# Experts of a mixture layer: the shared expert by chunks, the chosen one by gathered tiles

## The reference

```python
# Fourier attention, per head of 16 features
kv = jnp.cumsum(fft(k) * fft(v), axis=1)
vals = ifft(kv * conj(fft(q))).real ; return vals @ w_out
# mixture: swiglu(x, wg, wu, wd) = silu(x @ wg.T) * (x @ wu.T) @ wd.T, 128 -> 256 -> 128
shared_out = swiglu(x, shared_gate, shared_up, shared_down)
logits = x @ gate_w.T                        # 8 experts
top_id = argmax(logits) ; score = sigmoid(max(logits))
routed_out = sum over e of swiglu(where(top_id == e, x * score, 0), r_gate[e], r_up[e], r_down[e])
return shared_out + routed_out
```

## Time and profile before

| | |
|---|---|
| Median of 3 runs | 1799.72 us (1798.75 to 1801.79) |
| The profiled execution | 1799.19 us |
| its span | 1797.3 us |
| PE busy | 1580.2 us (88%) |
| DVE busy | 1324.0 us (74%) |
| ACT busy | 1146.9 us (64%) |
| POOL busy | 713.0 us (40%) |
| Mean granted clock of PE | 0.942 of full |

### The profile page before, as it was taken

One profiled execution on the slowest core, in us unless ns is written; L12 is line 12 of the kernel. 1 busy time (PEld: TensorE's weight loads), 2 busy tenths in 40 slices (PEclk: granted clock), 3 DMA queues, 4 the chain that ended last, 5 costly groups with the idle time before them and its releaser, 6 DMA issues. The chain is left out here.

```text
span 1797.3 us, 35515 instructions
## 1 busy us (share of the span) xinstructions
PE 1580.2 (88%) x8576; PEld 870.8 (48%) x8577; DVE 1324.0 (74%) x3585; ACT 1146.9 (64%) x2294; POOL 713.0 (40%) x1011
## 2 busy tenths in 40 slices
PE   2899999999999999999499999999498973799996
PEld 1333333333333333333277777777345552566664
DVE  2899999999999999998257666666347763466665
ACT  1387888888888888888466666666236553344342
POOL 2223344344443333322413333333135776144444
PEclk8699999999999999999799999999799985899998
DMA  3333332232323233221010000000120112222210
GB/s 110 75 96 100 86 95 79 81 89 77 93 80 87 79 93 95 72 55 31 13 65 1 1 0 0 0 0 1 27 71 16 44 48 97 72 59 59 59 55 17
DMA packets 84446, 102.48 MB, mean 57 GB/s; under 512 B 15995, under 2 KB 49537, under 8 KB 84368
## 3 DMA queue, kind: packets, MB, share of 16 engines
q1 hardware_dynamic: 78992, 88.89, 17.6%
q0 software_dynamic: 5376, 12.66, 2.0%
HBM read 61.44 MB, written 35.33 MB: 54 GB/s over the span
## 5 line engine op out<-in xcount | busy, mean ns | idle before, releaser
L827 DVE TENSOR_REDUCE bmax<-PS 128x8 f32<-128x512 f32 x1024 | 651.3, 683 | 61.4 <-PE PS L568 58.8
L678 ACT ACTIVATE EX<-PS 128x512 f32<-128x512 f32 x1024 | 565.2, 604 | 107.5 <-PE PS L579 97.9
L568 PE MATMUL PS<-KR,QR 33*128 33x512 f32 x1024 | 411.2, 469 | 50.4 <-DVE bmax L827 31.3
L579 PE MATMUL PS<-QR,KR 64*128 64x512 f32 x1024 | 399.1, 460 | 1.6 <-ACT EX L678 1.5
L568 PEld LDWEIGHTS PS<-KR,QR 33*128 33x128 f32 x1024 | 167.0, 188 | 366.6 <-DVE bmax L827 299.3
L589 PE MATMUL PS<-EX,VS 128*9 128x512 f32 x2048 | 268.6, 596 | 1.2 <-ACT EX L678 1.2
L579 PEld LDWEIGHTS PS<-QR,KR 64*128 64x128 f32 x1024 | 162.5, 185 | 11.3 <-ACT EX L678 10.2
L1024 PE MATMUL PS<-pA,wb 128*128 128x512 f32 x640 | 157.0, 401 | 0.0
L763 POOL TENSOR_TENSOR m_diff<-m_prev,m_all 128x16 f32<-128x16 f32 x64 | 14.2, 222 | 328.1 <-DVE m_all L839 328.1
L1853 ACT ACTIVATE g<-PS 128x512 f32<-128x512 f32 x72 | 43.0, 597 | 142.1 <-PE PS L1813 142.1
L1024 PEld LDWEIGHTS PS<-pA,wb 128*128 128x128 f32 x640 | 120.3, 191 | 27.5
(11 more groups left out here) (227 smaller groups left out, 2821.0 us busy)
## 6 DMA issues: line engine op xcount, KB each, us to landing
QR<-q_scr SPq DMA_DIRECT2D x256, 64.0 KB, 2.4
KR<-k_scr SPq DMA_DIRECT2D x256, 64.0 KB, 2.3
k_scr<-partsB SPq DMA_DIRECT2D x42, 256.0 KB, 2.9
rows<-row_scr SPq DMA_DIRECT2D x72, 129.0 KB, 2.1
q_scr<-partsB SPq DMA_DIRECT2D x28, 256.0 KB, 3.0
X<-in_L_attn_x SPq DMA_DIRECT2D x16, 256.0 KB, 3.0
X<-x SPq DMA_DIRECT2D x16, 256.0 KB, 2.4
xB<-in_L_attn_x SPq DMA_DIRECT2D x14, 256.0 KB, 3.3
```

The source lines that it names most:

```text
L568: pe.matmul(PS[:, bank_of(i, n), :], QR[rows, i, h // 2, t * P:(t + 1) * P], KR[rows, i, h // 2, :], start=True, stop=True).then_inc(tile_ ...
L579: pe.matmul(PS[:, RING3 + bank_of(j, n), :], KR[rows, j, h // 2, kt * P:(kt + 1) * P], QR[rows, j, h // 2, :], start=True, stop=True).then ...
L678: act.activation(EX[:, n % (2 * HG), :], PS[:, RING3 + bank_of(j, n), :], ACT.Exp, scale=SCALE).then_inc(ex_set, 1)
L827: dve.tensor_reduce(bmax[:, i % 2, n, :], PS[:, bank_of(i, n), :].rearrange("p (b k) -> p b k", k=BLK), AX_X, ALU.max).then_inc(tile_max, 1)
```

## The change

1. The rows in `row_scr` have 129 floats: the normalised token times its score, and its number. The score goes into a buffer of its own.
2. The chunk stage and the tile stage are one program. The normalised rows are written straight into AO, their transposes into XT (`copy_xT` waits for project's last matmul on it). xn4 and xT4 are gone.
3. The shared expert is computed by chunks of 512 tokens with its weights stationary, which gives the hidden features on the partitions, so that no transpose is needed before the down product. Chunks 0 to 7 (EARLY) stand at the end of steps 17 to 24 of the chunk stage's lists, chunks 8 to 15 behind the tiles. The result is copied into AO.
4. DVE's plan is called in step 22 of its list.
5. The tiles compute the chosen expert only: one transpose of rows, one expand, two transposes, two reduce matmuls, unrolled by 8. POOL scatters the bare result by token number into `y_scr` in DRAM.
6. A last pass in token order: SP loads y by chunks, DVE adds the shared result and takes statistics, POOL takes the power, ACT normalises, POOL adds x, SP stores.

The diff, cut to its core:

```diff
-    ROW = 2 * E + 2
+    ROW = E + 1
+    y_scr = nc.dram_tensor("y_scr", (TILES * P, E), F32).ap()
...
+        RING = 8
+        YRING = 4
+        EARLY = 8
+        SHARED_LAG = NCH + 1
...
 # SP
+                def load(j, k):
+                    r = sp.value_load(tile_row[0:1, ds(j, 1)], min_val=0, max_val=NE * REGION)
+                    if late(j, RING):
+                        sp.wait_ge(turned7, j - (RING - 1))
+                        sp.wait_ge(idx7_set, j - (RING - 1))
+                    sp.dma_start(rows7[:, k, :], row_scr[ds(r, P)]).then_inc(in7[k], 16)
+                run_stages(sp, ST_TILES, [(0, load)], RING)
+                def load_y(c):
+                    k = c % YRING
+                    if c >= YRING:
+                        sp.wait_ge(in7[YRING + k], ROWS_IN + c // YRING * 16)
+                    sp.dma_start(yr[:, k, :]..., y_chunks[:, c]).then_inc(in7[k], 16)
+                def store_out(c):
+                    sp.wait_ge(fin_set, c + 1)
+                    sp.dma_start(out_chunks[:, c], yr[:, k, :]...).then_inc(in7[YRING + k], 16)
+                sp.wait_ge(out5_done, NCH)
+                for k in range(4):
+                    sp.wait_ge(out7[k], ROWS_OUT)
+                for c in range(NCH + 2):
+                    if c < NCH:
+                        load_y(c)
+                    if c >= 2:
+                        store_out(c - 2)
...
 # PE
+                def shared_in(c):
+                    pe.wait_ge(xT4_set, c + 1)
+                    for f in range(FB1):
+                        if c:
+                            pe.wait_ge(hs_set, FB1 * (c - 1) + f + 1)
...
+                        pe.matmul(PS[:, 1 + 2 * f, :], sgu[:, f * P:(f + 1) * P], chunk_of(XT, c), ...)
+                        pe.matmul(PS[:, 2 + 2 * f, :], sgu[:, F1 + f * P:F1 + (f + 1) * P], chunk_of(XT, c),
+                                  start=True, stop=True).then_inc(gus_done, 1)
+                def shared_rows(c):
+                    pe.wait_ge(hs_set, FB1 * (c + 1))
...
+                    for t in range(NT):
+                        for f in range(FB1):
+                            mm = pe.matmul(PS[:, 5, t * P:(t + 1) * P], hs[:, c % 2, f, t * P:(t + 1) * P],
+                                           sdn[:, f, :], start=(f == 0), stop=(f == FB1 - 1))
+                    mm.then_inc(ys_done, 1)
...
-                run_stages(pe, NCH, [(0, project), (6, ranks), (4, turn), (1, combine), (2, output), (5, logits)])
+                run_stages(pe, NCH, [(0, project), (6, ranks), (4, turn), (1, combine), (2, output), (5, logits),
+                                     (SHARED_LAG, early(shared))])
+                shared_rows(EARLY - 1)
...
+                def expand(j, k):
+                    e = pe.value_load(tile_e[0:1, ds(j, 1)], min_val=0, max_val=NE - 1)
+                    pe.wait_ge(xT7_set, j + 1)
...
+                    pe.matmul(PS[:, GU_BANKS[s], :], xT7[:, s, :], wgu[:, ds(e * (2 * F1), 2 * F1)],
+                              start=True, stop=True).then_inc(gu7_done, 1)
...
+                run_stages(pe, ST_TILES, [(2, turn_x), (5, turn_h), (6, reduce), (3, expand)], RING)
+                pe.wait_ge(hT7_set, ST_TILES)
+                pe.wait_ge(o7_set, ST_TILES)
+                for c in range(EARLY, NCH + 1):
+                    if c < NCH:
+                        shared_in(c)
+                    if c > EARLY:
+                        shared_rows(c - 1)
...
 # ACT
                 def assemble(c, s):
-                    act.copy(row[:, s, :, 0:E], chunk_of(AO, c)...).then_inc(row_set, 1)
-                    act.copy(row[:, s, :, E:2 * E], chunk_of(X, c)...).then_inc(row_set, 1)
...
+                    act.activation(score[:, s, :], mx[:, s, :], ACT.Sigmoid).then_inc(row_set, 1)
+                    act.wait_ge(xn4_set, c + 1)
+                    act.wait_ge(row_set, c * ROW_STEPS + 2)
+                    for t in range(NT):
+                        act.activation(row[:, s, t, 0:E], tile_of(AO, c, t), ACT.Identity,
+                                       scale=score[:, s, t:t + 1]).then_inc(row_set, 1)
+                def shared_silu(c):
+                    for f in range(FB1):
+                        act.wait_ge(gus_done, FB1 * c + f + 1)
+                        if c:
+                            act.wait_ge(hs_set, FB1 * (c - 1) + f + 1)
+                        act.activation(gs[:, f, :], PS[:, 1 + 2 * f, :], ACT.Silu).then_inc(gs_set, 1)
+                def keep_shared(c):
+                    act.wait_ge(ys_done, c + 1)
...
+                    act.copy(chunk_of(AO, c), PS[:, 5, :]).then_inc(ys_kept, 1)
...
                 run_stages(act, NCH, [(0, copy_k), (3, out_rows), (0, copy_q), (6, copy_ranks), (4, copy_xT),
-                                      (5, copy_logits), (3, moe_rows), (6, assemble)])
+                                      (5, copy_logits), (3, moe_rows), (6, assemble),
+                                      (SHARED_LAG, early(shared))])
+                keep_shared(EARLY - 1)
...
+                run_stages(act, ST_TILES, [(2, copy_xT7), (5, copy_hT), (3, silus)], RING)
+                for c in range(EARLY, NCH + 1):
+                    if c < NCH:
+                        shared_silu(c)
+                    if c > EARLY:
+                        keep_shared(c - 1)
+                    if c > EARLY + 1:
+                        normalise(c - 2 - EARLY)
+                for c in range(NCH - 1 - EARLY, NCH):
+                    normalise(c)
...
 # POOL
+                run_stages(pool, ST_TILES, [(0, scatter_y)], RING)
+                def add_residual(c):
+                    pool.wait_ge(yn_set, c + 1)
+                    pool.tensor_tensor(yr[:, k, :], yr[:, k, :], chunk_of(X, c), ALU.add).then_inc(fin_set, 1)
+                for c in range(NCH + 1):
+                    if c < NCH:
+                        rstd(lnF[c % 2])(pool, c // 2)
+                    if c:
+                        add_residual(c - 1)
...
 # DVE
-                           + routing + [(2, lambda c, s: ln_bias(dve, c, lnC))])
+                           + routing + [(2, lambda c, s: ln_bias(dve, c, lnC)),
+                                        (NCH + 6, lambda c, s: plan() if c == 0 else None),
+                                        (SHARED_LAG, early(shared_gate))])
...
+                run_stages(dve, ST_TILES, [(6, take_y), (3, gate), (1, take_idx)], RING)
+                def final_stats(c):
+                    k = c % YRING
+                    dve.wait_ge(in7[k], ROWS_IN + c // YRING * 16 + 16)
+                    dve.wait_ge(ys_kept, c + 1)
+                    dve.tensor_tensor(yr[:, k, :], yr[:, k, :], chunk_of(AO, c), ALU.add).then_inc(ysum_set, 1)
+                    if c > 1:
+                        dve.wait_ge(yn_set, c - 1)
+                    dve.wait_ge(ysum_set, c + 1)
+                    ln_stats(dve, c // 2, lnF[c % 2], lambda t: yr[:, k, t * P:(t + 1) * P])
+                    ln_aggregate(dve, c // 2, lnF[c % 2])
+                    if c:
+                        ln_bias(dve, (c - 1) // 2, lnF[(c - 1) % 2])
+                for c in range(EARLY, NCH):
+                    shared_gate(c)
+                    if c > EARLY:
+                        final_stats(c - 1 - EARLY)
+                for c in range(NCH - 1 - EARLY, NCH):
+                    final_stats(c)
```

More of the change, by code:

```diff
@@ L1403, in block_kernel, with early, limited @@
         RB = 7
+        RING = 8
+        YRING = 4
+        EARLY = 8
+        SHARED_LAG = NCH + 1
+        rows7 = sb("rows7", [P, RING, ROW], F32, p5)
+        idx7 = sb("idx7", [P, RING], U32, p5)
+        xT7 = sb("xT7", [P, 2, P], F32, p5)
+        g7 = sb("g7", [P, 2, F1], F32, p5)
+        h7 = sb("h7", [P, 2, F1], F32, p5)
+        hT7 = sb("hT7", [P, 2, FB1, P], F32, p5)
+        o7 = sb("o7", [P, 4, E], F32, p5)
+        gs = sb("gs", [P, FB1, S], F32, p5)
+        hs = qq
+        yr = p34[:].rearrange("p a b s -> p (a b) s")
+        lnF = [ln_bufs("lnF0", p5, LN_SCALED), ln_bufs("lnF1", p5, LN_SCALED)]
+        in7 = [sem(f"in7_{k}") for k in range(RING)]
+        idx7_set = sem("idx7_set")
+        turned7 = sem("turned7")
+        xT7_set = sem("xT7_set")
+        gu7_done = sem("gu7_done")
+        g7_set = sem("g7_set")
+        h7_set = sem("h7_set")
+        h7_turned = sem("h7_turned")
+        hT7_set = sem("hT7_set")
+        y7_done = sem("y7_done")
+        o7_set = sem("o7_set")
+        out7 = [sem(f"out7_{k}") for k in range(4)]
+        ROWS_IN = ST_TILES // RING * 16
+        ROWS_OUT = ST_TILES // 4 * 16
+        gus_done = sem("gus_done")
+        gs_set = sem("gs_set")
+        hs_set = sem("hs_set")
+        ys_done = sem("ys_done")
+        ys_kept = sem("ys_kept")
+        ysum_set = sem("ysum_set")
+        yn_set = sem("yn_set")
+        fin_set = sem("fin_set")
+        ROUTE = 16
+        X_BANKS, H_BANKS, Y_BANKS, GU_BANKS = (0, 5), (1, 2), (3, 4), (6, 7)
```

(49 more changed lines are left out.)

317 lines of the change are left out of this document (119 added, 198 removed).

## The result

The changed kernel takes **1830.28 us** (median of 4 runs, 1829.14 to 1830.77), the kernel before 1799.24 us on the same chip (1797.83 to 1801.79). The ratio is 1.017, its 95% interval 1.0155 to 1.0184: slower by 1.7%. The forecast was 1812, slower by 0.7%. The span of the profiled run is 1828.8 us against 1797.3, with a mean granted clock of 0.942 in both, so a lower mean clock is no part of the difference.

A forecast was written before the change was run, and what follows sets the result against it. PE was taken to bound the 72 tiles at full clock. Tiles give back 104 us, chunk stage, tail and planning cost 25.5, the last pass +92: together +13, from 1799 to 1812 us; 8 in 10 range 1788 to 1834.

The forecast's parts named there:

- Step 1: Chunk stage, steps 6 to 15: ACT's assemble before copy_k grows from 1.35 to 2.0 us; +7 us, between 0 and +10.
- Step 2: Chunk stage's tail, steps 17 to 21, with shared chunks 0 to 4 and Sigmoid/Silu table loads: +9 us.
- Rival (d): Tail: each table switch costs its 1.28 us load once again, 12.8 us more, 1825 us; chance 0.03.
- Rival (b): Sigmoid and Silu share one table and step 1 is partly absorbed: 12 to 14 us less, 1798 to 1800; chance 0.13.
- 5.3 us stall: ACT's unexplained stall in the old tail, taken as instruction fetch; straight code would lose it, otherwise the sum is 5 higher.
- Step 3: From last place step to first routed tile: 25.6 us against 18.1, +7.5, and +2 for PE's clock.
- +2 for the clock: Planning, before the first routed tile: PE's clock taken to be at half in this stretch, +2 us.
- Step 4: The 72 tiles: 1.9 us each by PE's sequencer, 143 us against 247 before; ends 1.64 and 2.1.
- Rival (a): Tiles: PE's sequencer is hidden, a tile costs 1.64 us, 19.5 us less, 1792 us; chance 0.27.
- Step 5: New last pass in 16 chunks, after the last reduce: 105 us, between 80 and 130.
- Rival (c): Last pass: PE stays at half clock, a shared chunk costs 10 us in place of 6.5; +21, 1833 us; chance 0.17.
- +3.5 for the clock: Last pass, mixed rounds: PE busy under 80%, so part of it runs at half clock, +3.5 us.

The follow-up runs named there:

- e4: Changed kernel with Sigmoid in place of Silu in the first eight shared chunks, so no table switches in the tail; 1828.05 us, ratio 1.0148 to the kernel before.
- e5: Kernel before, with expert 0's weights for every tile so PE reads no expert number; 1797.72 us, ratio 0.9967 to the kernel before.
- e7: e3 with DVE's plan one step earlier and six shared chunks ahead of the tiles in place of eight; 1777.71 us, ratio 0.9852 to the kernel before.
- e1: Changed kernel with the expert-number read taken out of both expand and reduce; 1774.52 us, ratio 0.9852 to the kernel before.
- e2: Changed kernel with PE's list of tiles written out in full, both reads kept; 1816.61 us, ratio 1.0087 to the kernel before.
- e3: Changed kernel with PE's tile list written out and expand's number kept for reduce, one read a tile; 1777.02 us, ratio 0.9865 to the kernel before.

## Why the prediction was wrong in size

The direction came out, and the range held the time. The size did not: 0.7% forecast, 1.7% measured. In the span it is 1828.8 against 1810.6, 18.2 us, and the steps add up to it: -6.7, +0.5, -1.3, +33.3, -7.6.

**Step 1, chunk stage: forecast +7, measured +0.3.** The added wait and the order are as described, the price of the four activations was not. I took them from the four of moe_rows, 1.65 us, which have a bias and a scale. Those of assemble have a scale alone:

```profile
1461.49 1.28 ACT L1745 ACTIVATE row<-AO,score 128x128 f32<-128x128 f32 x4
1462.67 0.56 ACT L1693 COPY kA<-PS 128x512 f32<-128x512 f32 x1
```

1.28 in place of 1.65, so assemble takes 1.56 us to copy_k (with the id copy at 1461.11) where it was 1.35. The sum of PE's idle time before turn by ACT kA is 9.3 us in 7 cases from 1380 to 1460, 9.5 in 7 before. The lower end of my range, "if the waits absorb it", was the right one.

**Step 2, tail: forecast +9, measured +9.5.** Ten table loads of 1283 ns, as forecast. The timeline of ACT of one step:

```profile
1521.90 1.28 ACT L1741 ACT_TABLE_LOAD   x1
1523.20 0.20 ACT L1741 ACTIVATE score<-mx 128x4 f32<-128x4 f32 x1
1523.50 1.28 ACT L1745 ACTIVATE row<-AO,score 128x128 f32<-128x128 f32 x4
1524.79 1.28 ACT L1753 ACT_TABLE_LOAD   x1
1526.09 1.08 ACT L1753 ACTIVATE gs<-PS 128x512 f32<-128x512 f32 x2
```

The sum was right, its attribution half wrong. "Without the switches it is about 0" fell with e4: 5.9 of the 9.5 us stay, for PE's shared matmuls, which I had put beside ACT's chain, stand in the chain themselves. Rival (d), another 1.28 a switch, is refuted by the same rows: the load at 1524.79 ends at 1526.07 and the silu starts at 1526.09. The Trainium skill (ScalarE: Activation LUTs, What ACT_TABLE_LOAD costs) has 1283 ns and about 1380 for a drain; this trace agrees with the first, and with 0.01 us ahead of the load and 0.02 behind it there is no room for the second. Rival (b) is refuted by the ten loads.

The 5.3 us stall I read wrongly. The old tail has a second one, one step later, that I didn't count:

```profile
1517.85 0.19 ACT L1572 COPY rk<-PS 128x40 f32<-128x40 f32 x1 [4.26 <-remote]
```

The matmuls that the two copies wait for end at 1508.8 and 1513.9, so ACT is 3.4 and 3.9 us late. e5, the kernel before but for the reads, has both again (5.36 and 7.04). "Straight code would lose" them doesn't hold either: steps 16 to 21 stand written out behind the loop in the kernel before too, and ACT's last loop branch there is at 1470.2, so by the trace no branch stands near either stall. The Trainium skill (Runtime: NRT & Kernel Launch, Instruction fetch mechanics) has such a stall only for a taken branch whose target lies outside the window of code already fetched, a condition that I left out. The changed kernel and e4 have no such stall; why is open. Set against the old tail less 7.3 us of stalls, the shared chunks with their switches cost about 17 us and without them about 13, estimates from these rows. That the sum came to +9 is in part luck.

**Step 3, planning: forecast +7.5 and +2, measured +8.2.** The plan's first instruction starts 5.1 us behind the last place step (forecast 5.6), and the last keep is what comes late, as forecast. The timelines of DVE and of PE:

```profile
1528.79 0.17 DVE L1939 TENSOR_TENSOR filled<-filled,rk 128x8 f32<-128x8 f32 x1
...
1533.87 0.16 DVE L1967 CAST end_i<-filled 128x8 int32<-128x8 f32 x1
```

```profile
1555.14 0.41 PE L1636 MATMUL PS<-idf,rows 128*128 128x128 f32 x2 [0.87 <-ACT AO L1759]
```

The first transpose waits 0.87 us for ACT's last keep (L1759, 1554.30 to 1554.89). The +2 for the clock was wrong: with shared chunks in it PE runs at full clock from 1526 to 1555 (granted 1.00, busy 24.7 of 29). e7 shows that the rest can be had back.

**Step 4, tiles: the step that failed.** The forecast was "I take 1.9" us a tile, 143 us; measured are 176.3 us from the first transpose to the last reduce, 2.35 for each of the 75 steps, outside my ends of 1.64 to 2.1. The mechanism, two reads on PE's sequencer, is shown by e1, e2 and e3. Its size was read too low twice. I priced a read at 0.7 us, from distances of starts in the kernel before, and the time from the start of a load to its matmul is 0.94 and 0.98 in median; written out, the tile takes 2.18 (e2). And the loop, its return with the address work that hangs on its counter, had no term in my sum, for I named the steps that compute the slices' addresses and then gave them nothing; it is 0.23 a tile (e2). Rival (a), all hidden, was refuted: its 1.64 appears only where a read or both are gone (e1, e3).

There was a sign in the old profile that I took as covered: "PE never waits on a read in the trace". e5 shows 6.4 us of reads in that stage. PE busy 59.91 of 60 didn't exclude them, since the ends of matmuls in the record are modelled.

**Step 5, last pass: forecast 105, measured 97.4.** The structure came out: seven rounds in which shared chunks are mixed in, then the loop through SP's queue, a load 0.42 us behind each store. A mixed round took 5.9 us where I had 6.5 (3.0 us less in all), and the queue's loop 4.5 a chunk where I had 4.4. Rival (c), half clock in the mixed rounds, is refuted by the stretches 1740 to 1776 and 1776 to 1829 of the changed kernel (the number behind POOL's is the clock):

```profile
1740.00:1776.00 36.00, 33.68 (x159) 21.53 (x158) 21.51 (x79) 18.24 (x39) 12.47 (x11) 1.00 0.22 60
1776.00:1829.00 53.00, 1.49 (x14) 1.30 (x12) 21.28 (x110) 18.47 (x45) 24.05 (x21) 0.56 0.37 103
```

PE is busy 33.7 of 36 us at 1.00; the clock falls to its half level only when its matmuls are over and nothing depends on it (0.56 is the mean of 1776 to 1829). My +3.5 for the clock was wrong too, and makes up nearly half of this step's error; the end behind the last sum was some 2 us shorter than forecast.

Steps 1 and 5 were priced too dear by 6.7 and 7.6 us, which hid part of what step 4 lacked: with these two right, the forecast would have been farther off.

**Where the expected gain went.** Measured in the changed kernel, the tiles give back 70.8 us and the rest costs 102. With one read and no loop (e3) the tiles give back 125, and the same change is 1.3% faster than the kernel before. What is left of its cost is above all the last pass, 84 us longer than the old end: seven rounds with shared chunks, whose matmuls the tiles no longer have, and then the chunks that go through SP's queue with PE idle.

## What to carry to other kernels

When a change halves the matmuls of a loop's round, write down what the engine's sequencer does in that round, instruction by instruction from the start of the read to the matmul that uses it, before trusting the matmuls' sum; bringing a number from SBUF into a register and using it took about 1 us here, so read once and keep it. Where every engine is under 80% busy and the releasers name different engines, replace the run-time value by a constant in one run: it settles whether the data or the control holds the loop. In a queue that both loads and stores, a load right behind a waiting store starts only when that store's chunk is done; storing one slot later gave 0.7 us a chunk here.

## What the runs showed of the hardware

- A value read from SBUF on PE's sequencer: 0.30 us for the load itself, 0.94 and 0.98 (medians of expand and reduce) from its start to the matmul whose address depends on it. Two such reads hold a round at 2.18 us written out, 2.41 in a loop.
- The return of the loop of eight slots shows as 3.2 us between expands where others stand 2.34 to 2.55 apart.
- ACT on 128x128 f32 from SBUF to SBUF, 64 times each: 0.39 us with a scale alone, 0.48 with bias and scale.
- Sigmoid and Silu, used in turns, load a table every time, 1283 ns, and the next activation starts 0.02 us behind it.
- A group of three kernels on one chip had tiles of 125 to 131 us where the same instructions took 122 in another group. The cause is open.
- In the old tail ACT stood idle for 5.33 and 4.26 us ahead of two copies whose matmuls were done 3.4 and 3.9 us before them (in e5 5.36 and 7.04 us of idle time); the changed kernel has no such stall. The cause is open.
